# Block 0 of the next stage summed and normed at the end of the mixture of experts, and the late shared expert in another order

## The reference

```python
x = x + 0.5 * _L0_ffn_ref(_layernorm(x), ...)   # 32 experts, 4 per token, capacity 160, and a shared expert
x = x + _L0_attn_ref(_layernorm(x), ...)        # gated linear attention, chunks of 128, 8 heads
x = x + 0.5 * _L0_ffn_ref(_layernorm(x), ...)   # the same mixture again, on the new x
x = x + 0.5 * _L1_ffn_ref(_layernorm(x), ...)   # 8 experts, 2 per token, bfloat16
x = x + _L1_attn_ref(_layernorm(x), ...)        # token shift, decaying state
x = x + 0.5 * _L1_ffn_ref(_layernorm(x), ...)
```

```python
shared = silu(x @ shared_gate.T) * (x @ shared_up.T) @ shared_down.T
```

## Time and profile before

| | |
|---|---|
| three runs | 1153.76, 1155.86, 1157.72 us, median 1155.86 |
| profiled execution | 1156.85 us, of which the span of the trace is 1154.9 |
| busy share of the span | PE 89%, PEld 52%, DVE 63%, ACT 48%, POOL 33% |
| granted TensorE clock, mean | 0.946 of 2.4 GHz |
| end of ffn0a, first instruction of `project` | near 246 us |
| end of ffn0b, first instruction of `ffn1a` | near 748 us |

### The profile page before, as it was taken

The page is one execution under the profiler, slowest core; times in us unless marked ns, Lnnn a source line. Parts: engine busy times, 40 slices in busy tenths (PEclk is TensorE's granted clock), DMA queues, the critical chain, the costliest instruction groups (busy, mean ns, idle before and its releaser), DMA issues. The chain is left out here.

```text
span 1154.9 us, 17176 instructions
## 1 busy us (share of the span) xinstructions
PE 1023.1 (89%) x5110; PEld 606.1 (52%) x5128; DVE 723.8 (63%) x2529; ACT 560.0 (48%) x1071; POOL 383.0 (33%) x448
## 2 busy tenths in 40 slices
PE   7998899969998799989998989857887799985997
PEld 4755666535565466656666666423333456642343
DVE  4598432147884566754797331168876699964885
ACT  6621333325665745548422333246664655525884
POOL 3006777700000232314017887311101256521110
PEclk9999899999999799999999999968889899997998
DMA  9849987834440802005428887575400000000012
GB/s 326 331 159 306 185 199 182 183 113 146 151 141 13 324 37 91 11 28 173 165 73 157 201 234 132 104 230 181 141 5 1 1 0 1 1 1 0 20 54 73
DMA packets 81127, 140.72 MB, mean 122 GB/s; under 512 B 17776, under 2 KB 48864, under 8 KB 78944
## 3 DMA queue, kind: packets, MB, share of 16 engines
q1 hardware_dynamic: 65696, 117.58, 29.4%
q0 software_dynamic: 15360, 22.29, 13.0%
HBM read 82.17 MB, written 58.72 MB: 122 GB/s over the span
## 5 line engine op out<-in xcount | busy, mean ns | idle before, releaser
L693 POOL DMA_INDIRECT ffn_sums<-ffn0a_xT,ffn0a_into x40 | 62.7, 1567 | 16.0 <-issue 8.8
L693 POOL DMA_INDIRECT ffn_sums<-ffn0b_xT,ffn0b_into x40 | 62.5, 1563 | 14.7 <-issue 9.2
L1721 POOL TENSOR_TENSOR attn_attend_state_m<-attn_attend_state,attn_attend_heads 128x512 f32<-128x512 f32 x15 | 19.1, 1272 | 87.3 <-DVE attn_attend_state L1763 81.8
L2593 PE MATMUL attn_ps_k<-attn_xk,mixing_wk 128*128 128x512 f32 (+1 forms) x96 | 46.7, 610 | 0.0
L2598 PE MATMUL attn_ps_r<-attn_xr,mixing_wr 128*128 128x512 f32 (+1 forms) x96 | 45.2, 593 | 0.7 <-DVE attn_out L2462 0.7
L1143 DVE TENSOR_TENSOR ffn0a_h<-ffn0a_sg,ffn0a_ps_b 128x160 f32<-128x160 f32 x32 | 10.3, 322 | 54.4 <-ACT ffn0a_sg L981 54.3
L2608 PE MATMUL attn_ps_y<-mixing_wv,attn_out 128*128 128x256 f32 (+1 forms) x192 | 43.0, 380 | 1.2 <-DVE attn_out L2462 1.2
L842 PE MATMUL ffn0a_ps_b<-main_x,ffn0a_h 128*32 128x256 f32 (+2 forms) x144 | 43.5, 403 | 0.0
L842 PE MATMUL ffn0b_ps_b<-main_x,ffn0b_h 128*32 128x256 f32 (+2 forms) x144 | 43.5, 403 | 0.0
L820 PE MATMUL ffn0a_ps_b<-ffn0a_early,main_x 128*128 128x160 f32 x256 | 41.3, 305 | 2.1 <-DMA main_x<-w_experts 1.8
L1742 DVE COPY_PREDICATED main_spare<-attn_attend_causal,attn_attend_ps_a 128x1024 f32<-128x1024 int32 x32 | 40.3, 1312 | 4.6 <-issue 3.0
(11 more groups left out here) (510 smaller groups left out, 2718.9 us busy)
## 6 DMA issues: line engine op xcount, KB each, us to landing
main_spare<-ffn_sums SPq DMA_DIRECT2D x128, 256.0 KB, 3.6
main_x<-w_experts SPq DMA_DIRECT2D x16, 1536.0 KB, 7.1
ffn_sums<-main_lent SPq DMA_DIRECT2D x36, 512.0 KB, 6.3
ffn_sums<-main_x SPq DMA_DIRECT2D x28, 512.0 KB, 4.6
ffn_rows<-ffn0a_early SPq DMA_DIRECT2D x8, 512.0 KB, 9.7
ffn_rows<-ffn0b_early SPq DMA_DIRECT2D x8, 512.0 KB, 2.9
x_out<-main_x SPq DMA_DIRECT2D x8, 512.0 KB, 2.9
main_x<-x_in SPq DMA_DIRECT2D x3, 1024.0 KB, 10.7
```

Source lines behind the costliest of these rows:

```text
L693: g.indirect_dma_start(out=sums[:, :], out_offset=IndirectOffsetOnAxis(ap=into[:, at, j:j + 1], axis=0), in_=ys[:, n % NY, :], in_offset=N ...
L2593: ins = mm(ps_k[0:rows, m % 2], wk[:, k, at:at + rows], xk[:, p, k, :], start=k == 0, stop=k == KD - 1)
```

## The change

It does four things, at both seams between a mixture and the stage behind it.

1. The late shared expert: TensorE does the up products of both late blocks, then the down products of both. ScalarE's order follows.
2. Block 0 of the next stage is summed (`dve_first`, now in three calls), measured and normed by VectorE and GpSimd inside the mixture's block. The three sums stand between VectorE's last products for the late expert. The normed rows go into tiles 28 to 31 of `main_x`. SyncE issues the copies of block 1 (`combine.sp(1)`) there too. In `ffn1a` VectorE norms block 0 now, not ScalarE; the class `NormWithShift` holds what was `norm` in that stage.
3. The next stage begins with block 0's transposes. In `project` the joining of the gate weights stands around them, and ScalarE's table load is moved into the mixture, between its last SiLU and its last copies. In `ffn1a` the cast of constants stands behind block 0's two copies and the table load is gone.
4. The warm-up products at the start of `project` and of `ffn1a` are gone (those of `ffn1b` stay).

```diff
@@ -205,6 +205,17 @@
...
+    def place(self, sc, ps_t):
+
+        self.ps_t = ps_t
+        if self.xn is None:
+            self.xn = sc.sb("ln_xn", [P, 2, self.nt, D])
+        if self.whole_xT is None:
+            self.xT = sc.sb("ln_xT", [P, 2, KD, self.nt * P])
+
+    def xn_of(self, b, p):
+        return self.first_xn if isinstance(b, int) and b == 0 and self.first_xn is not None else self.xn[:, p]
...
+class NormWithShift(Norm):
...
+    def pool_start(self):
+        self.nc.gpsimd.memset(self.minus[:], -1.0).then_inc(self.minus_set, 1)
+        self.nc.gpsimd.wait_ge(self.minus_set, 1)
+        super().pool_start()
+
+    def pool(self, j):
+        (b, p, i), g = j, self.nc.gpsimd
+        g.wait_ge(self.moments_ready, b + 1)
+        g.tensor_tensor(self.ve[:, p, :], self.moments[:, p, :, 1], self.eps[:], ALU.add).then_inc(self.ve_ready, 1)
+        after(g, self.shift_ready, b)
+        g.tensor_tensor(self.neg_mean[:], self.moments[:, p, :, 0], self.minus[:], ALU.mult)
+        g.wait_ge(self.ve_ready, b + 1)
+        after(g, self.xn_ready, b - 1)
+        g.tensor_tensor(self.rstd[:, p, :], self.ve[:, p, :], self.power[:], ALU.pow).then_inc(self.rstd_ready, 1)
+        g.wait_ge(self.rstd_ready, b + 1)
+        g.tensor_tensor(self.shift[:, p, :], self.neg_mean[:], self.rstd[:, p, :], ALU.mult)\
+            .then_inc(self.shift_ready, 1)
...
@@ -662,6 +703,7 @@
                     for piece in range(ends - (NADD if n == 0 else 1), ends):
                         sp.wait_ge(*landed(piece))
                     combine.sp_first(n)
+                combine.sp(1)
 
...
@@ -716,6 +758,8 @@
                     add(n)
                     if 6 <= n < 6 + SA:
                         index.pool(3, range(n - 6, n - 5), xg[3], table, gathered)
+                head.pool_start()
+                head.pool(number(0))
...
-                def down(n, half, ps=ps_y):
+                def down(n, half, ps=ps_y, banks=1):
                     pe.wait_ge(h_made, 2 * n + 2)
-                    after(pe, y_kept, 2 * n + half)
+                    after(pe, y_kept, 2 * n + half + 1 - banks)
...
                         up(n, m, late_ps[m])
+                for n in range(NF, NB):
                     for half in range(2):
-                        down(n, half, late_y[half])
+                        down(n, half, late_y[half], banks=2)
...
                     for m in range(2):
                         gate(n, m, late_ps[m])
+                if next_table:
+                    s.preload_act_table_set(next_table)
+                for n in range(NF, NB):
                     for half in range(2):
                         keep_late(n, half, late_y[half])
...
                 dve.wait_ge(piece_made, NP)
-                for n in range(NF, NB):
-                    for m in range(2):
-                        hidden(n, m, (ps_a, ps_b[:, 0:2])[m])
+                late_ps = (ps_a, ps_b[:, 0:2])
+                hidden(NF, 0, late_ps[0])
+                hidden(NF, 1, late_ps[1])
+                combine.dve_first(1)
+                hidden(NF + 1, 0, late_ps[0])
+                combine.dve_first(2)
+                hidden(NF + 1, 1, late_ps[1])
+                combine.dve_first(3)
+                head.dve_moments(number(0), lambda t: t)
+                head.dve_apply(number(0), lambda t: t)
...
-    def dve_first(self):
+    def dve_first(self, n):
 
         v, parts = self.nc.vector, self.parts
-        v.wait_ge(self.first_landed[0], 32)
-        v.wait_ge(self.first_landed[1], 32)
-        v.tensor_tensor(parts[:, :, 0], parts[:, :, 0], parts[:, :, 1], ALU.add).then_inc(self.first_step, 1)
-        v.wait_ge(self.first_step, 1)
-        v.wait_ge(self.first_landed[2], 32)
-        v.tensor_tensor(parts[:, :, 0], parts[:, :, 0], parts[:, :, 2], ALU.add).then_inc(self.first_step, 1)
-        v.wait_ge(self.first_step, 2)
-        v.wait_ge(self.first_landed[3], 32)
+        if n == 1:
+            v.wait_ge(self.first_landed[0], 32)
+        else:
+            v.wait_ge(self.first_step, n - 1)
+        v.wait_ge(self.first_landed[n], 32)
+        if n < NTAB - 1:
+            v.tensor_tensor(parts[:, :, 0], parts[:, :, 0], parts[:, :, n], ALU.add).then_inc(self.first_step, 1)
+            return
         for half in range(2):
             rows = self.x[:, half * (BT // 2):(half + 1) * (BT // 2), :]
-            v.tensor_tensor(rows, parts[:, half, 0], parts[:, half, 3], ALU.add).then_inc(self.added, 2)
+            v.tensor_tensor(rows, parts[:, half, 0], parts[:, half, n], ALU.add).then_inc(self.added, 2)
         v.wait_ge(self.added, 4)
         v.memset(self.waiter[:], 0.0)
...
-                for b in range(1, NB):
+                for b in range(2, NB):
                     combine.sp(b)
...
-                ln.pool_start()
-                each(pool, ln.pool, NB)
+                each(pool, ln.pool, NB, 1)
...
                     dve.wait_ge(carry_set, 2)
-                    combine.dve_first()
-                    ln.dve_moments(j, lambda t: j[0] * BT + t)
-                    ln.dve_apply(j, lambda t: j[0] * BT + t)
                     combine.dve((1, 1, 0), 0)
...
-                s.preload_act_table_set(EXP_AND_LN)
                 act.wait_ge(weights, 8 * 16)
                 act.wait_ge(w1_turned, 1)
                 s.activation(w1T, ps_kd[0:LOW, 0:KD, :], ACT.Copy).then_inc(w1T_kept, 1)
-                act.wait_ge(w12_made, 1)
-                s.activation(w12, ps_z[:, 0:KD * HK].rearrange("p (k n) -> p k n", k=KD), ACT.Copy)\
-                    .then_inc(w12_kept, 1)
-                act.wait_ge(ln.power_set, 1)
 
                 def first(j):
                     ln.act(j)
+                    act.wait_ge(w12_made, 1)
+                    s.activation(w12, ps_z[:, 0:KD * HK].rearrange("p (k n) -> p k n", k=KD), ACT.Copy)\
+                        .then_inc(w12_kept, 1)
 
                 rounds(act, first, work, NB)
                 keep_kd(NB - 1)
@@ -1573,22 +1622,19 @@
                     ins.then_inc(kd_turned, 1)
 
                 def first(j):
-                    ln.pe(j)
-                    pe.wait_ge(w12_kept, 1)
-                    pe.wait_ge(v_centred, 3)
-
-                def join_gate_weights():
+
                     pe.wait_ge(weights, 8 * 16)
                     for k in range(KD):
                         ins = nc.tensor.transpose(ps_kd[0:LOW, k, :], w1[:, k, :], con[:, C_IDENT:C_IDENT + P])
                     ins.then_inc(w1_turned, 1)
+                    ln.pe(j)
                     pe.wait_ge(w1T_kept, 1)
                     for k in range(KD):
                         ins = mm(ps_z[:, k * HK:(k + 1) * HK], w1T[:, k, :], w2[:], start=True, stop=True)
                     ins.then_inc(w12_made, 1)
-
-                join_gate_weights()
-                warm(nc, con, ps_t[:, 0, :], 5)
+                    pe.wait_ge(w12_kept, 1)
+                    pe.wait_ge(v_centred, 3)
+
                 rounds(pe, first, work, NB)
                 turn_kd(NB - 1)
...
-                g = nc.gpsimd
-                g.memset(minus[:], -1.0).then_inc(minus_set, 1)
-                pool.wait_ge(minus_set, 1)
-                ln.pool_start()
-
...
+                if not head:
+                    ln.pool_start()
+                each(pool, ln.pool, NB, 1 if head else 0)
...
-                if combine:
-                    combine.dve_first()
-                moments(number(0))
+                if not head:
+                    moments(number(0))
                 if combine:
                     combine.dve(number(1), 0)
                     combine.dve(number(1), 1)
...
-                s.preload_act_table_set(SILU)
-                if combine:
-                    ew.cast_constants()
-                act.wait_ge(ln.power_set, 1)
-                apply(number(0), 0)
-                apply(number(0), 1)
+                if not head:
+                    s.preload_act_table_set(SILU)
+                if not head:
+                    apply(number(0), 0)
+                    apply(number(0), 1)
                 turned(number(0))
                 turned16(number(0))
+                if head:
+                    ew.cast_constants()
                 keep_raw(number(0))
                 staged(act, work, NB)
...
-                warm(nc, con, ps_t[:, 0, :], 5 if combine else 3)
+                if not head:
+                    warm(nc, con, ps_t[:, 0, :], 3)
                 ln.pe(number(0))
                 score(number(0))
                 pe.wait_ge(ew.constants_cast, 1)
...
+        block0_xn = x[:, NT - BT:NT, :]
+        with Scope(nc, "attn0_head") as held:
+            head = Norm(held, nc, x, con, BT, first_xn=block0_xn)
+            moe(nc, "ffn0a", x, con, w, table, sums, gathered, added, 0, spare, combine[0], head,
+                (con_landed, x_landed, load_x, spare_set, start_spare_rows), gw.load, zero=lent[:, 0:BT * D],
+                next_table=EXP_AND_LN)
```

(3 more changed lines are left out.)

73 lines of the change are left out of this document (32 added, 41 removed).

## The result

| | median of the runs | runs | ratio to the kernel before, 95% interval |
|---|---|---|---|
| before | 1156.11 us | 9 | |
| changed | 1144.07 us (1139.65 to 1151.65) | 9 | 0.9893 [0.9862, 0.9925] |

The change gains 12 us. 22 were forecast, with a range of 1128 to 1142, so the result lies outside. The profiled execution of the changed kernel took 1151.65 us (span 1149.4): it is the slowest of the nine, so positions are compared from the late expert's first up product on, and not from the start.

The account below looks back on a forecast made before the run. The prediction took stages ending in common barriers to bound the kernel, with TensorE's largest standstills at two seams. Gains of 12.3 + 9.9 = 22.2 us took 1156.85 to 1134.6, the median to 1133.7, stated as 1134; range 1128 to 1142.

Parts of the forecast that it names:

- Barrier + 0.26: First seam: the next stage starts 0.26 us after the last engine, VectorE, at 243.5 instead of 246.35, gain 2.85.
- rival A: Both mixture ends: VectorE's tail ends later behind late copies, two to three us per seam, 1139; chance 0.12.
- VectorE's chain: First seam: block 0's last additions to end of norm take 6.05 us, from 237.2 to 243.25, ending last.
- From the barrier on: Next stage: first z product 3.9 us after the start, 12.3 earlier overall; block 1 has 4.3 us of slack.
- The second seam's end: Last tables land at 741.4, the chain ends at 747.5, the next stage starts at 747.75, 0.3 us earlier.
- The waits that the new order saves TensorE are not the gain: Mixture ends: the removed wait, 2.8 us at each seam, only keeps TensorE off the path, since VectorE ends last.
- Rival E: Early sums wait until the barrier and only the late expert's waits go: gain 0 to 5 us, 1153; chance 0.04.
- The clock, cost 0: Behind the first seam: TensorE spends the same 5 us at the lower clock as today, cost 0 either way.
- bound of -2.5: Behind the first seam: the clock's best case, full clock from the stage's start, worth 2.5 us.
- B: Behind the seams: block 0 is early but block 1 is not, price some 9 us, 1143; chance 0.08.
- C: Both seams: the clock comes back sooner, up to 5 us more gain, 1129; chance 0.13.
- D: Projection: without warm-up TensorE stays long at 1.2 GHz; two rounds make it 5 us slower, 1161; chance 0.03.

Follow-up runs that it names:

- e2_early_drain: The changed kernel with one more GpSimd drain after its last scatter and memsets, ahead of its wait for block 0's moments, at both seams: 1132.56 us, 0.9788 of before.
- e1_copies_back: The changed kernel with block 1's eight copies moved back to the start of the next stage, at both seams: 1149.53 us, 0.9947 of before.
- f2_head_alone: e2_early_drain with the late experts' products back in the order of before (up, down, up, down), at both seams: 1136.60 us, 0.9844 of before.
- f1_order_alone: The kernel before with only the late shared experts' order changed, both up products and then both down products, at both seams: 1142.61 us, 0.9888 of before.
- f5_three_warm: e2_early_drain with three warm-up products on TensorE behind the late experts' last down product, at both seams: 1131.74 us, 0.9808 of before.

## Why the prediction was wrong, and where it was right

**The step that failed: "Barrier + 0.26".** The prediction took the barrier to follow the last engine by 0.26 and named VectorE as the last engine. In its working GpSimd appears only as VectorE's wait of 1.51 for the power, and rival A just says that GpSimd's new work stands in front of the barrier too. The prediction did not ask what GpSimd has to do after its last operation. Measured in that place: 251.66 - 246.57 = 5.1 at the first seam and 751.39 - 746.04 = 5.35 at the second, 9.9 us more than forecast together. 22.2 - 9.9 = 12.3, measured 12.0. e2_early_drain takes away nothing but this and lands at 1132.6 (and 1134.3 on another chip) where 1134 was forecast. The trace of before held the drain, 13.9 us long, but only in the view of the block's own line, which the prediction does not use. (In the changed kernel's profiled execution the four stretches of the table are together 10.4 shorter than before: there another 1.8 us is missing, by which VectorE's norm ended late, 1.1 and 0.7.)

**VectorE's chain: right.** Its end was forecast 24.0 us behind the first up product (243.25 - 219.26). It is at 25.1 in the changed kernel's profiled execution, where the copies landed later (the additions stand behind a wait for them of 0.67), and at 23.9 in e2_early_drain's (its norm 240.50 + 1.38, its first up product 217.93). Four up steps of 3.5 from 219.26 end at 233.3, not at 233.1; nothing hangs on it.

**From the barrier on: right.** The z product was forecast 3.9 behind the stage's start: 255.58 - 251.66 = 3.9. Block 1 is on time: TensorE's transposes at 267.14 have no wait ahead of them. Only the second seam loses time without the early copies (e1_copies_back). The stages became 9.0 and 9.9 us shorter, forecast 9.4 and 9.6 (12.3 less 2.85; 9.9 less 0.3).

**The second seam's end: right in kind.** Forecast 26.5 behind the first up product; the norm's end is at +27.2 in the changed kernel, where the last scatter starts at +10.7, and at +23.7 in e2_early_drain, where it starts at +6.7.

**"The waits that the new order saves TensorE are not the gain": right of this kernel only.** There VectorE's norm ends behind TensorE and ScalarE, as computed, and the order keeps these off the path: with the order of before each end is 3.5 us longer (f2_head_alone). Without block 0's norm in the mixture TensorE and ScalarE are the last engines, and the order alone brings the same 1.1% (f1_order_alone). Rival E priced this case, "only the waits of the late expert go", at 0 to 5 us; it measured 12.7, of which the two ends are 10.8.

**The clock, cost 0: right against before, too little for what it could be.** The z product ran at 0.50, 3.78 us, before 3.75. TensorE's wait at the barrier was taken as 2.5; it was 8.02 with the drain on the path and 3.20 in e2_early_drain. The bound of -2.5 for full clock was too small: stage 1 showed 3 to 4 us. The Trainium skill (TensorE: Matmul & The Clock Gate, "What's actually happening") has it that activity releases the throttle; the trace of f5_three_warm agrees, with 1.00 in the 10 us behind the barrier after three products that nothing reads, and 0.52 without.

**The rivals.** None names the drain. A's consequence is right, a barrier later than computed (its sign, "a barrier at 246 or 748 and later", is there), but its mechanism, late copies ahead of VectorE's chain, is 1.8 us of the 11.7 that are missing there. B's 1143 is the nearest time, and that is chance: block 1 was not late. C, D and E did not come about; against D, the granted clock is 1.00 from 10 to 20 us behind the first barrier.

## What to carry to other kernels

Before work of an engine is moved behind its last instruction in a block, read that engine's drain, which the timelines leave out: a drain that ended 10 us ahead of the barrier costs nothing, and the same drain behind a late 0.1 us operation is the critical path. If the engine idles before the late operation, a drain of its own there takes the price off. And of two edits that are made together, time each alone: here the order alone brought as much as both together, and the early norm needed a line more to bring its own.

## What the runs showed of the hardware

- GpSimd's drain takes 0.08 us for each indirect DMA that GpSimd issued since its last drain: 0.38 us at 4, 1.69 at 20, 6.2 at 80, and 0.05 to 0.07 at none. It counts from GpSimd's last operation, even where the last transfer had landed 12.8 us ahead of it. One plain DMA of 32 KB added some 0.1 us. SyncE's outstanding copies do not hold the drain or the barrier.
- Stage 1 took 113.4 to 113.9 us in the six profiled executions in which the granted clock was 1.00 in its first 10 us, and 117.3 to 117.6 in the four in which it was 0.50 to 0.52. Ahead of it TensorE had stood idle 1.42 us (f2_head_alone, 1.00) or 3.20 us (e2_early_drain, 0.52); three warm-up products (2.74 us) in that wait gave 1.00.
